# The second expert layer's GpSimd queue: one scatter and one gather in turn, in place of two gathers and two scatters

## The reference

```
x = layernorm(x).reshape(2048, 256)
probs = softmax(x @ router_w)                     # 32 experts
topk_w, topk_idx = top_k(probs, 4);  topk_w = topk_w / sum(topk_w)
combine = sum(one_hot(topk_idx, 32) * topk_w)
g = einsum('th,ehi->tei', x, w_gate);  u = einsum('th,ehi->tei', x, w_up)      # i = 192
eo = einsum('tei,eih->teh', silu(g) * u, w_down)
out = x_in + tanh(g_ffn) * (einsum('te,teh->th', combine, eo) + shared_expert)
```

## Time and profile before

| | us |
|---|---|
| median of 3 runs (lowest, highest) | 1305.9 (1297.75, 1308.65) |
| the profiled execution, its own time | 1307.36 |
| span of its instructions | 1305.6 |
| mean granted TensorE clock of the span | 0.975 |
| PE busy | 1233.9 (95% of the span) |
| DVE busy | 759.3 (58%) |
| ACT busy | 666.9 (51%) |
| POOL busy | 689.5 (53%) |
| the loop over the 80 tiles, from its first transposes to its last `down` | 1052.5 to 1268.6 |
| the combine | 1268.6 to 1305.6 |

### The profile page before, as it was taken

How to read it: one execution, slowest core, us unless ns; L and a number is a source line. 1 busy time by engine, 2 the same in 40 slices (tenths; PEclk the granted TensorE clock), 3 DMA queues, 4 the chain that set the end, 5 groups by cost and what they waited for, 6 DMA issues and landing times. The chain is left out here.

```text
span 1305.6 us, 26094 instructions
## 1 busy us (share of the span) xinstructions
PE 1233.9 (95%) x9183; PEld 936.2 (72%) x9184; DVE 759.3 (58%) x1547; ACT 666.9 (51%) x1511; POOL 689.5 (53%) x686
## 2 busy tenths in 40 slices
PE   4999897999999999999999998999799989999986
PEld 3677656888888888888888885677565655555545
DVE  6787675444445454444444426777659646566654
ACT  2877854554555455455455436766332135555543
POOL 5565305566655655566666444333016737777750
PEclk9999998999999999999999998999879999999998
DMA  7334343444444444455544539100220058888868
GB/s 258 53 60 63 58 146 112 99 105 106 108 106 103 91 88 99 111 112 112 112 109 107 127 65 332 59 8 2 71 92 1 13 154 242 245 247 247 236 173 322
DMA packets 139031, 161.72 MB, mean 124 GB/s; under 512 B 79141, under 2 KB 104363, under 8 KB 137648
## 3 DMA queue, kind: packets, MB, share of 16 engines
q1 hardware_dynamic: 104656, 106.23, 27.3%
q0 software_dynamic: 32256, 52.46, 19.7%
q10 hardware_dynamic: 2016, 1.71, 0.4%
HBM read 122.60 MB, written 39.85 MB: 124 GB/s over the span
## 5 line engine op out<-in xcount | busy, mean ns | idle before, releaser
L1402 POOL DMA_INDIRECT x_dram<-e_y,rows x128 | 217.4, 1699 | 191.0 <-ACT e_y L1511 165.7
L1546 DVE TENSOR_TENSOR e_hid<-e_sg,bank 128x512 f32<-128x512 f32 x128 | 88.1, 688 | 129.0 <-PE bank L1437 95.4
L1498 ACT CAST e_hidden_hi<-e_hid 128x512 fp32r<-128x512 f32 x128 | 79.5, 621 | 162.0 <-DVE e_hid L1546 162.0
L1437 PE MATMUL bank<-e_xg_hi,e_w_hi 128*128 128x512 f32 x512 | 159.0, 392 | 2.0 <-issue 2.0
L1340 POOL DMA_INDIRECT spare<-xn_dram,rows x128 | 125.0, 976 | 66.2 <-issue 38.4
L1437 PE MATMUL bank<-e_xg_hi,e_w_lo 128*128 128x512 f32 x512 | 158.6, 391 | 0.0
L1437 PE MATMUL bank<-e_xg_lo,e_w_hi 128*128 128x512 f32 x512 | 158.4, 391 | 0.0
L1549 DVE TENSOR_TENSOR e_hidden_lo<-e_hid,e_hidden_hi 128x512 fp32r<-128x512 f32 x128 | 88.6, 692 | 88.0 <-ACT e_hidden_hi L1498 88.0
L2102 PE MATMUL bank<-w,e_xT 128*64 128x384 f32 x320 | 112.5, 495 | 6.2 <-issue 3.2
L1511 ACT ACTIVATE e_y<-bank,shares 128x256 f32<-128x256 f32 x128 | 60.8, 475 | 105.3 <-PE bank L1450 105.0
L2102 PE MATMUL bank<-e_wt,e_xT 128*64 128x384 f32 x320 | 113.6, 499 | 0.0
(11 more groups left out here) (330 smaller groups left out, 2631.7 us busy)
## 6 DMA issues: line engine op xcount, KB each, us to landing
w<-in_L_ffn_w SPq DMA_DIRECT2D x48, 512.0 KB
kT<-in_L_down SPq DMA_DIRECT2D x108, 192.0 KB
wgu<-in_L_gate_up SPq DMA_DIRECT2D x8, 1536.0 KB, 9.5
V<-in_L_down SPq DMA_DIRECT2D x52, 192.0 KB
kT<-ys_dram SPq DMA_DIRECT2D x4, 1024.0 KB, 7.9
xn_dram<-V SPq DMA_DIRECT2D x5, 512.0 KB, 11.0
X<-in_x SPq DMA_DIRECT2D x4, 512.0 KB, 10.0
b_cT<-in_ctx_p SPq DMA_DIRECT2D x4, 512.0 KB, 13.0
```

What stands on the lines that cost most here:

```text
L1402: nc.gpsimd.indirect_dma_start(out=x_dram[:, :], out_offset=bass.IndirectOffsetOnAxis(ap=rows[:, e, q:q + 1], axis=0), in_=y[q][:, :], in_ ...
L1437: last = nc.tensor.matmul(bank[f % 2][:, :], w[:, k * F0 + f * 128:k * F0 + (f + 1) * 128], x[:, k, h * SLOTS:(h + 1) * SLOTS], start=(w, ...
L1498: nc.scalar.copy(hidden[0][:, f, :], hid[f % 2][:, :]).then_inc(hi_sb, 1)
L1546: nc.vector.tensor_tensor(hid[f % 2][:, :], sg[f % 2][:, :], U_BANK[f % 2][:, :], ALU.mult).then_inc(hid_sb, 1)
```

## The change

In the loop of `experts1_phase` on GpSimd, the two gathers and two scatters of each turn are replaced by one scatter and one gather in turn, the scatter first. The same 80 scatters and 72 gathers are issued, with the same waits.

```diff
-            for t in range(0, PAIRS, 2):
-                for u in (t, t + 1):
-                    if u + NXT < PAIRS:
-                        gather(u + NXT)
-                for u in (t, t + 1):
-                    scatter(u)
+            for t in range(PAIRS):
+                scatter(t)
+                if t + NXT < PAIRS:
+                    gather(t + NXT)
```

## The result

The changed kernel takes 1340.25 us (median of 4 runs, 1335.08 to 1349.65) against 1301.83 us (median of 4, 1297.17 to 1308.65): the ratio is 1.0293, with a 95% interval of 1.0246 to 1.0339. It is slower, as forecast, by 38 us where 27 were forecast. Timed again in the experiments it took 1338.59 us, ratio 1.0288 (1.0214 to 1.0362).

The account below looks back on a forecast made before the run. TensorE was taken to bound the kernel; the change closes a ring of 5.15 + 4.6 + 2.3 = 12.05 us against 10.56 for two turns, so 18 x 1.49 = 26.8 us on 1305.9 gives 1333 us, range 1316 to 1347.

Parts of the forecast that it names:

- TensorE sets the pace before: Loop between the result copies of tiles 0 and 72: TensorE busy 98% of 190.00 us, at most 3.2 us to gain.
- gather(t+9) starts 5.15 us after it: GpSimd's queue: 1.23 us to the scatter, then 3.92 us for scatter, gather, scatter; the start was 0.58 us before.
- the 18 rings: Copy, scatters, gather, landing, transposes, next copy: 12.05 us against 10.56 for two turns, 18 times, costing 26.8 us.
- The landing of 4.6 us: Time from a loop gather's start until its data has landed, bracketed from the earlier trace; likely band 4.0 to 5.3 us.
- 2.3 us from the transposes to the next result copy: From the start of tile t+9's transposes on TensorE to tile t+4's result copy on VectorE: 2.3 us.
- The rings of the odd turns: The same chain begun at tiles 2, 6, ... 74 runs beside the first at the same pace, adding nothing.
- Longer gathers, up to 5 us: Gathers on GpSimd taking 1.29 instead of 0.99 us may add up to 0.3 us a ring, 5 us in all.
- B: Rival: the ring binds only a little because landings shorten; 1311 us at a landing of 3.4 us; chance 0.11.
- C: Rival: not slower at all, with landings of 3.1 us or less; 1303 to 1306 us; chance 0.04.
- D: Rival: TensorE's clock falls too as its holes grow to about 14% of the loop; 1345 to 1360 us; chance 0.05.
- The forecast of 217 us between the two copies: Forecast time from the result copy of tile 0 to that of tile 72, which took 190.00 us before.

Follow-up runs that it names:

- e4: The changed kernel's order with ten gather buffers instead of eight, tiles 8 and 9 gathered at the loop's head: 1300.06 us, ratio 0.9995.
- e8: The changed kernel once more, unaltered, for a second profile: 1338.59 us, ratio 1.0288.
- e10: The changed kernel with three idle matmuls between the transposes of tiles t+4 and t+5, in every second turn alone: 1340.46 us, ratio 1.0286.
- e3: The changed kernel reordered half way, one scatter ahead of the turn's two gathers and one behind: 1323.07 us, ratio 1.0168.
- e5: The changed kernel without 148 of 160 loads of down weights (output wrong): 1310.07 us, ratio 1.0053 to the kernel before.
- e9: The changed kernel with each gather behind one scatter more, scatter(t) then gather(t+7): 1472.16 us, ratio 1.1299.
- e6: The kernel before without 148 of 160 loads of down weights (output wrong): 1306.39 us, ratio 1.001.
- e1: The changed kernel with one gather and one scatter in turn, but the gather first: 1308.53 us, ratio 1.0034.
- e2: The changed kernel not in turn: both scatters of a turn first, then its two gathers: 1339.87 us, ratio 1.0317.
- e7: The changed kernel with three idle matmuls between the transposes of tiles t+4 and t+5, in every turn: 1343.72 us, ratio 1.0339.

## Why the prediction was right, point by point

- **TensorE sets the pace before, and there is at most 3 us to gain.** Right. With all slack restored the new order took 189.03 us against 190.00 (e4), and its time didn't differ from before.
- **The scatter waits for its copy, and gather(t+9) starts 5.15 us after it.** Right to the hundredth at the head of the loop (1054.87 to 1060.02). Averaged over the 18 rings from the copy of tile 0 on it was 5.25 us (5.33 in e8). The scatter itself started 1.22 us after its copy in each ring; the excess comes from two rings, one with a scatter of 1.36 us and one in which the gather of tile 60 began 1.82 us behind its scatter instead of 0.30. That pause stands ahead of tile 60's gather in e8, e10 and e3 too; what it is, was not found.
- **The landing of 4.6 us.** Right: 4.5 at the median, 4.57 averaged over these 18 gathers, and 4.15 in e8 (by its semaphore updates). The choice between the earlier trace rows was the one that decided the sign, and e5 shows why it had to be the second: 2.8 us is the landing without the loop's weight loads. The prediction chose by the DMA share, and that reason was weaker than the choice: e9 has the share of the first layer (0.46 against 0.47) and a landing of 4.0. By the fit in the Trainium skill's "DMA: Bandwidth & Descriptors", section "Anatomy of one DMA — SWDGE (gpsimd) path", an estimated 2.3 us, the change would have been free. This trace doesn't agree with it: the quickest landing that the profile of the changed kernel tells took 3.1 us.
- **2.3 us from the transposes to the next result copy.** Too small, and the term that was mis-sized most. It was read from a single good turn (2.38 us in the earlier trace rows) and shortened by 0.1. Averaged over 36 turns the same distance was 2.54 us in the kernel before, and in the changed one 2.55, or 2.66 over the 18 rings. The register loads ahead of VectorE's weight copies take 0.3 to 0.8 us and the one good turn had short ones; and in three rings the clock's falls lengthened the distance, 2.5 us in all (e10 above). 18 x 0.36 = 6.5 us, with these 2.5 in it, of the 8.8 that the loop's forecast lacked (225.6 against 190.0 + 26.8); most of the rest is the 0.10 us at the gather's start, 1.8 us.
- **The rings of the odd turns run beside and are not added.** Not added, but not quite free. In e8 the three averages make 5.33 + 4.15 + 2.55 = 12.03 us, and the ring took 222.50 / 18 = 12.36. The missing 0.33 us is TensorE's: in three of the 18 rings (tiles 37, 41 and 77) it came to the transposes 0.55, 1.43 and 3.23 us after the landing, and in each case the turn before, one of the other ring, had waited for its own gather (3.03 us for tile 75's). TensorE goes by the slower of the two rings, so a sum of the averages of one falls short.
- **Longer gathers, up to 5 us.** They exist (up to 1.34 us). Where it is gather(t+9) itself, the landing as measured holds it; one ahead of it in the queue is in the gather's start, and there a scatter of 1.36 us cost 0.34 us once. Nothing like 5 us is left for them.
- **The rivals.** B and C (short landings) are what e5 and e6 made on purpose; with the loads in place they didn't come. D came in a small form: the clock was 0.98 in the loop, with holes of up to 2.9 us where the forecast said under 2. It cost about 2.5 us there and 1.0 in e8, nothing that e10's time could show.
- **The range.** 1316 to 1347 holds 1340. Of the 38 us between the medians the loop accounts for 35.6 by the first profile of the changed kernel and 32.5 by e8. The kernel before also read 4 us faster in the result than in the forecast (1301.83 against 1305.9), with one more execution in the median; its executions lie in two groups (last section). The forecast of 217 us between the two copies was 6 to 9 us short, and the combine came out longer in the first profile (52.93 us from tile 72's copy to the end, 49.26 before) but not in e8 (49.51).

## What to carry to other kernels

An in-order queue that issues both prefetches and write-backs makes each prefetch wait for whatever the write-back ahead of it waits for; count the prefetch's slack from that event, not from the queue's idle time. Write the loop that this closes as a sum (event, scatter, gather, landing, consumer, event) and compare it with as many turns as the buffers allow: here 12.0 to 12.5 against 10.56 us, and one pair of buffers more makes it 15.8. Take the landing from that very stage, with its own transfers running beside it, and the consumer's steps as an average over many turns.

## What the runs showed of the hardware

- **The landing of one 128 KB gather goes from 2.8 to 4.5 us when the loop's weight loads run beside it,** and not by the mean DMA share alone. With the loads it was 4.5 us at the median in e4 (share 0.88), 4.4 in e1 (0.85), 4.5 in the changed kernel (0.75) and still 4.0 in e9 (0.46), with single ones up to 6.5 (e2). Without them it was 2.8 in e5 (0.30) and 3.0 in e6 (0.31), and 2.8 in the first layer (0.47).
- **Executions of one program fall into two groups 10 us apart, by a stretch at 1.2 GHz ahead of the loop.** All 13 timed executions of the kernel before beside e9 lie at 1296.0 to 1298.5 us with a mean clock of 0.983 to 0.987, or at 1305.6 to 1311.8 with 0.973 to 0.978. In the first profile of before TensorE ran at half clock in the routing stage for 27.3 us from 935.90 on, in that of the changed kernel for 6.8 us from 934.73 on. The 13 profiles here divide the same way: with the short stretch (the changed kernel, e2, e5, e7) the first result copy comes at 1054.9 to 1058.8, with the long one of 27 to 31 us (the other nine) at 1062.8 to 1066.5. The changed kernel had the long stretch too, in e8, so it is not the change that decides. That the two groups of unprofiled times are these two stretches is inferred from their mean clocks. The stretches of those two first profiles (columns as in the earlier trace rows; the second window begins 0.1 us late):

```profile
935.90:963.21 27.31, 22.80 (x99) 21.34 (x100) 11.07 (x28) 5.75 (x9) 2.80 (x10) 0.50 0.52 194
```

```profile
934.83:941.66 6.83, 3.36 (x16) 3.36 (x17) 4.62 (x13) 1.38 (x3) 2.80 (x10) 0.51 0.55 169
```

  What decides between them, the runs don't tell. A comparison of two single profiles can be off by these 10 us.
- **The clock fell at holes of 2 to 3 us in otherwise full turns, but not at each of them.** In the changed kernel's loop it fell three times, twice for 3.4 us and once for 6.8, at holes of 2.17, 2.07 and 2.85 us, and a `down` of 1.53 us then took up to 2.84. Holes of 2.32 and 2.24 us in the same loop, of 2.62 in e8 and of 2.59 in e2 brought no fall. In e9, where TensorE waited 2.1 to 4.7 us in each of 35 turns of 9 to 11.6 us, it fell 29 times.
- **Leaving the weight loads out did not make the old order's loop faster:** 193.10 us in e6 against 190.00 and 189.77, with the DMA share down from 0.88 to 0.31. TensorE's busy time is the same (186.17 us against 186.02), so the 3 us are idle time; why there is more of it was not found.
